# Six transformer layers on one NeuronCore: a loop over layers with two stages becomes one pipeline of 202 steps, and the softmax's maxima and sums are handled in another way

## The reference

```python
def local_attention(q, k, v):          # windows of 32 rows, each sees itself and the one before
    ...
    mask = (it < jb) | (it > jb + w) | (jb == -1)
    sim = jnp.einsum('bhwie,bhwje->bhwij', bq, bk2) * QK_SCALE
    sim = jnp.where(mask, -jnp.finfo(sim.dtype).max, sim)
    attn = jax.nn.softmax(sim, -1)
    out = jnp.einsum('bhwij,bhwje->bhwie', attn, bv2)

def attn_layer(x, Wqkv, qs, ksc, Wo):  # 16 heads of 64
    q, k, v = jnp.split(x @ Wqkv, 3, -1)
    ...
    q = l2norm(q) * qs
    k = l2norm(k) * ksc
    q = q * cos * scale + rotate_half(q) * sin * scale
    k = k * cos * inv + rotate_half(k) * sin * inv
    return local_attention(q, k, v) @ Wo           # (heads put side by side)

def ffn_layer(x, g, bln, W1, b1, W2, b2):          # 341 hidden columns and as many gates
    xn = (x - mu) / jnp.sqrt(var + 1e-05) * g + bln
    a, gate = jnp.split(xn @ W1 + b1, 2, -1)
    return a * jax.nn.gelu(gate, approximate=False) @ W2 + b2

for i in range(6):
    x = attn_layer(shift_tokens(x), ...) + x
    x = ffn_layer(shift_tokens(x), ...) + x
```

## Time and profile before

| | |
|---|---|
| three runs, median (lowest to highest) | 3576.26 us (3575.43 to 3576.86) |
| the profiled execution | 3575.57 us, its span 3573.7 us |
| mean granted TensorE clock | 0.958 of full speed |
| PE busy | 3252.6 us, 91% |
| ACT busy | 2933.6 us, 82% |
| DVE busy | 2791.6 us, 78% |
| POOL busy | 2045.7 us, 57% |
| exponentials (L1321), busy of instruction and accumulator read | 1229.9 and 765.0 us, 3072 each |

### The profile page before, as it was taken

The page is one execution under the profiler, slowest core; times in us unless marked ns, Lnnn a source line. Parts: engine busy times, 40 slices in busy tenths (PEclk is TensorE's granted clock), DMA queues, the critical chain, the costliest instruction groups (busy, mean ns, idle before and its releaser), DMA issues. The chain is left out here.

```text
span 3573.7 us, 118257 instructions
## 1 busy us (share of the span) xinstructions
PE 3252.6 (91%) x42076; PEld 2208.0 (62%) x42076; DVE 2791.6 (78%) x5370; ACT 2933.6 (82%) x9257; POOL 2045.7 (57%) x2150
## 2 busy tenths in 40 slices
PE   5699998889999789999789999978999977999977
PEld 4466665656666556666566666665666655666656
DVE  7788887578888568888658888757888856888865
ACT  3399998479999459999649999937999955999973
POOL 3566665456666356666446666545666634666644
PEclk8799999899999899999899999989999989999999
DMA  2000001100000100000110000010000010000011
GB/s 70 10 7 8 7 7 33 22 13 7 7 7 6 47 15 8 7 7 7 37 24 7 8 7 7 10 44 14 7 8 7 6 43 19 8 7 7 7 34 42
DMA packets 141061, 57.58 MB, mean 16 GB/s; under 512 B 118598, under 2 KB 137668, under 8 KB 139460
## 3 DMA queue, kind: packets, MB, share of 16 engines
q1 hardware_dynamic: 140484, 50.01, 5.9%
HBM read 22.57 MB, written 2.10 MB: 7 GB/s over the span
## 5 line engine op out<-in xcount | busy, mean ns | idle before, releaser
L1321 ACT ACTIVATE probs<-s_ps,nbias,rnorm 128x64 f32<-128x64 f32 x3072 | 1229.9, 447 | 1.6 <-DVE nbias L1039 0.9
L1524 POOL TENSOR_TENSOR qk_rot<-by_cos,by_sin 128x1024 f32<-128x1024 f32 x384 | 914.0, 2380 | 381.9 <-DVE by_sin L989 334.8
L597 PE MATMUL ring<-wvo,xsT 128*32 128x512 f32 x6144 | 794.8, 600 | 10.2 <-ACT vo L1144 10.2
L1321 ACT ACTIVATION_READ_ACCUMULATOR probs<-s_ps,nbias,rnorm 128x1 f32 x3072 | 765.0, 249 | 0.0
L1513 POOL TENSOR_TENSOR probs<-probs,rrow 128x256 f32<-128x256 f32 x768 | 454.6, 613 | 429.1 <-DVE rrow L973 429.1
L986 DVE TENSOR_TENSOR by_cos<-qk_ps,rotary 128x1024 f32<-128x1024 f32 x378 | 463.0, 1225 | 147.1 <-ACT squares L1307 147.1
L1533 POOL TENSOR_TENSOR qk_rot<-qk_rot,rnorm 128x1024 f32<-128x1024 f32 x192 | 365.5, 1904 | 341.4 <-DVE rnorm L733 341.4
L543 PEld LDWEIGHTS ring<-cst,qk_rot 128*128 128x128 f32 x3072 | 341.3, 141 | 243.7 <-ACT vo L1144 155.9
L543 PE MATMUL ring<-cst,qk_rot 128*128 128x128 f32 x3072 | 446.4, 278 | 27.6 <-POOL qk_rot L1524 24.4
L1001 DVE TENSOR_REDUCE sumsq<-squares 128x16 f32<-128x1024 f32 x384 | 462.9, 1206 | 0.0
L989 DVE TENSOR_TENSOR by_sin<-qk_ps,rotary 128x1024 f32<-128x1024 f32 x378 | 459.2, 1215 | 0.0
(11 more groups left out here) (166 smaller groups left out, 5433.4 us busy)
## 6 DMA issues: line engine op xcount, KB each, us to landing
qk_rot<-L_ffn_Wqkv SPq DMA_DIRECT2D x7, 1024.0 KB, 5.1
xs<-x_tok SPq DMA_DIRECT2D x194, 32.0 KB
xs<-x_tok SPq DMA_DIRECT2D x194, 31.8 KB
by_cos<-x_tok SPq DMA_DIRECT2D x48, 128.0 KB
by_cos<-x_tok SPq DMA_DIRECT2D x48, 127.0 KB
wv<-L_ffn_Wqkv SPq DMA_DIRECT2D x7, 512.0 KB, 6.6
wo_pad<-L_ffn_Wo SPq DMA_DIRECT2D x14, 256.0 KB, 7.3
xs<-x_tok SPq DMA_DIRECT2D x194, 0.2 KB
```

What stands on the lines that cost most here:

```text
L597: last = mm(r[WIN * mh:WIN * (mh + 1), :], xsT[:, a, WIN * w:WIN * (w + 1)], wvo[:, mh, :, :], start=True, stop=True)
L1321: last = nc.scalar.activation(probs[:, a, h // 4, :, h % 4, :], s_ps[:, half, c:c + 2 * WIN].rearrange("p (s c) -> p s c", s=2), ACT.Exp, ...
L1524: g.tensor_tensor(qk_rot[:, n, :], by_cos[:, n, :], by_sin[:, n, :], ALU.add).then_inc(added[qk], 1)
```

## The change

The loop over layers goes, and so does the border between the two stages. One list of 202 steps per engine covers 6 x 32 tiles; a tile's attention is spread over steps k to k+3, and the feed-forward work of a group of four tiles is set into the steps that follow its last tile (group(k, f) is the group whose last residual was f steps ago). The next layer's weights are prepared in the steps at the end of the layer before, in buffers of their own (wqk_next, wvo_odd and wvo_even, w1_hi, w1_lo). Layer norm's gain goes into W1 and its offset into the bias b1 (bias_product, biases); group squares are made on POOL (squared4), Gelu writes into hid. All four vo copies and all kT copies are ACT's now. q is scaled by 1/|q| on POOL (normalise_rotated "q"), so that exponentials need no scale; the negated maxima (float32r) are added to the scores by a PE product (shift), and so they need no bias: an instruction takes four heads, 4 a tile. Row sums are reductions on DVE (row_sums). The mask is added in PSUM by DVE (in maxima), except for the first tile of a sequence, which still has a PE product.

The core of the diff; the feed-forward parts keep the operations of before but for what is said above.

```diff
+TILES = DEPTH * NT
+GROUPS = DEPTH * NG
+LAST_RESIDUAL = FT - 1 + 3
+STEPS = LAST_RESIDUAL + FT * (GROUPS - 1) + 8
...
+        def group(k, f):
+
+            u, rest = divmod(k - LAST_RESIDUAL - f, FT)
+            return u if rest == 0 and 0 <= u < GROUPS else None
...
+        NEXT_VALUES = (("wvT0", 14), ("wvT1", 15), ("wvo0", 18), ("wvo1", 19), ("wvo2", 22), ("wvo3", 23))
+
+        def ring_uses(k):
+
+            groups_first = [("b1", layer_at(k, 7)), ("down", group(k, 6)), ("gate2", group(k, 3))]
+            groups_first += [(part, next_layer_at(k, at_step)) for part, at_step in NEXT_VALUES]
+            tiles_first = [("vo2", k - 2), ("qT1", k - 2), ("qT0", k - 2), ("vo1", k - 2), ("kT0", k - 2)]
+            groups_up = [("up0", group(k, 3)), ("up1", group(k, 3))]
+            tiles_next = [("vo0", k - 2), ("kT1", k - 2), ("pT0", k - 3), ("xsT", k)]
+            groups_next = [("xn", group(k, 2)), ("up2", group(k, 4))]
+            tiles_last = [("pT1", k - 3), ("vo3", k - 2), ("o", k - 3)]
+            groups_last = [("gate0", group(k, 2)), ("gate1", group(k, 2))]
+
...
-                every_tile(step, 3)
...
+                    if first:
+                        mm(s_ps[:, half, :], ident_bf[:, :],
+                           mask_bf[:, 0:2 * WIN].unsqueeze(1).broadcast_to([P, 8, 2 * WIN]),
                            start=True, stop=False, skip_group_check=True)
...
+                def shift(half, s):
+
+                    if not there(k, None, s):
+                        return
+                    T = T0 - s
+                    pe.wait_ge(max_done[half], done(T))
+                    mm(s_ps[:, half, :], ident_r[:, :], nmax[:, 8 * half:8 * half + 8].unsqueeze(2)
+                       .broadcast_to([P, 8, 2 * WIN]), start=False, stop=True,
+                       skip_group_check=True).then_inc(shifted[half], 1)
...
+                bias_product(layer_at(k, 7))
+                down(group(k, 6))
+                up("gate", 2, group(k, 3))
+                project("k", 0, 1)
+                project("k", 1, 1)
+                for part, at_step in NEXT_VALUES:
+                    next_values(next_layer_at(k, at_step), part)
+                values(2, 2)
+                transposed("q", 1, 2)
+                transposed("q", 0, 2)
+                values(1, 2)
+                transposed("k", 0, 2)
+                up("up", 0, group(k, 3))
+                up("up", 1, group(k, 3))
+                values(0, 2)
+                transposed("k", 1, 2)
+                probs_transposed(0, 3)
+                xs_transposed(0)
+                scores(0, 2)
+                normalised_transposed(group(k, 2))
+                project("q", 0, 0)
+                project("q", 1, 0)
+                up("up", 2, group(k, 4))
+                probs_transposed(1, 3)
+                values(3, 2)
+                scores(1, 2)
+                shift(0, 2)
+                output(3)
+                up("gate", 0, group(k, 2))
+                up("gate", 1, group(k, 2))
+                shift(1, 2)
+            every_step(step)
...
+                def row_sums(half, s):
+
+                    if not there(k, None, s):
+                        return
+                    T, a, h = T0 - s, (par - s) % 2, slice(8 * half, 8 * half + 8)
+                    dve.wait_ge(exp_done[half], done(T))
+                    p = probs[:, a, 2 * half:2 * half + 2].rearrange("p q s h c -> p q h s c")
+                    v.tensor_reduce(psum_row[:, h].rearrange("p (q h) -> p q h", q=2), p, AXY,
+                                    ALU.add).then_inc(row_summed[half], 1)
+
...
-                        T = T0 - s
-                        dve.wait_ge(s_ready[half], done(T))
-                        v.tensor_reduce(smax[:, 8 * half:8 * half + 8], heads(s_ps[:, half, :], 8), AX,
-                                        ALU.max).then_inc(max_done[half], 1)
...
+                    dve.wait_ge(shifted[half], done(T - 1))
+                    dve.wait_ge(s_ready[half], done(T))
+                    scored = heads(s_ps[:, half, :], 8)
+                    if T % TPB:
+                        v.tensor_tensor(scored, scored, mask_bf[:, 2 * WIN:4 * WIN].unsqueeze(1)
+                                        .broadcast_to([P, 8, 2 * WIN]), ALU.add).then_inc(masked[half], 1)
+                        dve.wait_ge(masked[half], passed(T - T // TPB))
+                    v.tensor_reduce(nmax[:, 8 * half:8 * half + 8], heads(s_ps[:, half, :], 8), AX, ALU.max,
+                                    negate=True).then_inc(max_done[half], 1)
...
+                x_new(group(k, 6))
+                biases(layer_at(k, 7))
+                sum_of_squares("k", 1)
+                row_reciprocals(1, 3)
+                inverse_norms(0, 1, 1)
+                rotate("k", 0, 1)
+                inverse_norms(1, 2, 1)
+                hidden(0, group(k, 3))
+                hidden(1, group(k, 3))
+                rotate("k", 1, 1)
+                xsT_lower(0)
+                normalised(group(k, 2))
+                centre(group(k, 1))
+                inverse_norms(2, 4, 1)
+                maxima(0, 2)
+                inverse_norms(4, 6, 1)
+                hidden(2, group(k, 4))
+                lower(group(k, 2))
+                inverse_norms(6, RSQRT_OPS, 1)
+                rotate("q", 0, 0)
+                maxima(1, 2)
+                rotate("q", 1, 0)
+                row_sums(0, 2)
+                residual(3)
+                group_deviation(group(k, 1))
+                row_reciprocals(0, 2)
+                w1_lower(layer_at(k, 7))
+                sum_of_squares("q", 0)
+                row_sums(1, 2)
+            every_step(step)
...
-                        for h in (h0, h0 + 1):
-                            c = h % 8 * 2 * WIN
-                            last = nc.scalar.activation(
-                                probs[:, a, h // 4, :, h % 4, :],
-                                s_ps[:, half, c:c + 2 * WIN].rearrange("p (s c) -> p s c", s=2), ACT.Exp,
-                                scale=rnorm[:, a, h:h + 1], bias=nbias[:, h:h + 1],
-                                accum_out=psum_row[:, h:h + 1])
...
+                    act.wait_ge(pT_ps[half], done(T - 2))
+                    act.wait_ge(shifted[half], done(T))
+                    for q in range(2):
+                        last = nc.scalar.activation(
+                            probs[:, a, 2 * half + q].rearrange("p s h c -> p h s c"),
+                            s_ps[:, half, 256 * q:256 * q + 256].rearrange("p (h s c) -> p h s c", h=4, s=2), ACT.Exp)
+                    last.then_inc(exp_done[half], 1)
+
...
+                gelu(group(k, 3))
+                square("k", 1)
+                next_wqk_upper(next_layer_at(k, NT), 1)
+                vo_evacuated(2, 2)
+                w1_upper(layer_at(k, 7))
+                for part, at_step in NEXT_VALUES:
+                    next_values(next_layer_at(k, at_step), part)
+                q_evacuated(1, 2)
+                q_evacuated(0, 2)
+                vo_evacuated(1, 2)
+                k_evacuated("low", 0, 2)
+                k_evacuated("high", 0, 2)
+                vo_evacuated(0, 2)
+                xsT_upper(0)
+                k_evacuated("low", 1, 2)
+                p_evacuated(0, 3)
+                k_evacuated("high", 1, 2)
+                normalised_upper(group(k, 2))
+                square("q", 0)
+                next_wqk_upper(next_layer_at(k, NT - 1), 0)
+                p_evacuated(1, 3)
+                xsT_evacuated(0)
+                exponentials(0, 2)
+                vo_evacuated(3, 2)
+                exponentials(1, 2)
+            every_step(step)
...
+
+                normalise(1, 2)
+                add_rotated("q", 0)
+                next_wqk_lower(next_layer_at(k, NT - 1), 0)
+                squared4(group(k, 0))
+                normalise_rotated("q", 0)
+                add_rotated("k", 0)
+                x_and_bias(group(k, 2))
+                normalise_rotated("k", 0)
+                group_rsqrt(group(k, 0))
+                normalise(0, 1)
+                next_wqk_lower(next_layer_at(k, NT - 1), 1)
+                for j in range(TPB):
+                    next_table(next_layer_at(k, NT - TPB + j + 1), j)
+            every_step(step)
```

More of the change, by code:

```diff
@@ L31 @@
 AX = mybir.AxisListType.X
+AXY = mybir.AxisListType.XY
 P = 128
@@ L89, in constants @@
     first[0:WIN, 0:WIN] = NEG
-    parts["mask"] = np.concatenate([first] + [mask] * (TPB // 2 - 1), 1)
-    parts["keep"] = np.tile((np.arange(TPB // 2) > 0).astype(f)[None], (P, 1))
+    parts["mask"] = np.concatenate([first, mask], 1)
     h = np.arange(P) // D0
@@ L316, in schedule, with every_step, there @@
                 step(k, k % 2, None)
-        def every_tile(step, depth, before_last=None):
-            for k in range(NT + depth):
-                if before_last and k == NT + depth - 1:
-                    before_last()
```

(56 more changed lines are left out.)

1350 lines of the change are left out of this document (628 added, 722 removed).

## The result

The changed kernel takes 3738.0 us (median of 4 runs, 3734.9 to 3739.5) where the kernel before takes 3576.5: ratio 1.045, 95% interval 1.043 to 1.047. It is slower by 162 us, and 304 us over the forecast of 3434. The profiled execution has a span of 3735.3 us.

What follows compares the result with a forecast made beforehand. PE was taken as full, with waits on DVE and ACT making 66.5 us per group of four tiles. 48 groups 3192, front 148, borders 60, ends 32 and 1.9 around the span gave 3434 us; range 3240 to 3600.

Steps and rivals of the forecast that it cites:

- plain: Step without feed-forward products on PE: 14.4 us, with PE idle 0.45 while DVE masks, takes maxima and rotates q.
- up 2: Step with feed-forward product up2 (f = 4): like the step without such products plus 0.75 us, 15.1.
- down, xn, gates: Step with down, xn and two gates: 18.5 us on PE plus 0.8 waiting for normalised, 19.3.
- gate 2, up 0, up 1: Step f = 3: 16.2 us on PE plus 1.5 idle behind ACT's Gelu table load and three Gelus, 17.7.
- PE, 13.95 a tile and 63.3 a group: PE's work at old product prices: 13.95 us a tile, plus 7.5 feed-forward per four tiles, 63.3 a group.
- Rival 4: DVE and POOL shut each other out of SBUF, 2.38 us per meeting, one in two tiles: 3660 us; chance 0.12.
- The other waits, 3.2 a group: PE's idle time within a group: 0.45 in steps waiting on DVE, 0.8 for normalised, 1.5 behind ACT's Gelus.
- the forecast's third step: Step f = 3, with gate2, up0 and up1: products wait for ring banks held behind hidden 0 and 1; 1.5 us idle.
- If PE waits longest for ring banks with ACT behind them: Sign that the forecast is wrong: the copies moved to ACT would then be the cost; no size given.
- Rival 3: DVE's mask and row sums at their upper end, 0.6 us more in 7 tiles of 8: 3535 us; chance 0.05.
- Table loads: ACT's two loads a group, 1.28 us each: Gelu's delays the f = 3 step, Exp's fits in ACT's spare time.
- Borders at 12 each: Five layer borders at 12 us, 60 in all, for values, transposes, weight parts and project's waits of about 1 and 4.5.

Runs made afterwards that it cites:

- e4: The changed kernel with POOL's sum of q split into four instructions of 256 columns, DVE's order untouched: 3583.6 us, ratio 1.0025.
- e6: The kernel before with values 0 and the four transposes of k swapped, adding two changes of kind per tile: 3624.5 us, ratio 1.014.
- e12: e7 with k's first half taken first by PE and ACT, and all four POOL passes over q and k in quarters: 3778.3 us, ratio 1.056.
- e11: e4 with half of the output's products left out (output not the reference's): 3510.0 us, 74 less than e4.
- e7: e5's product order, with e4's quartered sum and the norm's blocked int32 step moved ahead of k's first rotation: 3574.0 us, ratio 0.9998.
- e3: The changed kernel with the mask added by PE products in all tiles and none by DVE: 3761.2 us, ratio 1.052.
- e8: e7 with Identity in place of Gelu, so no table loads for it (output not the reference's): 3522.6 us, 51 less than e7.
- e5: The changed kernel with PE's products grouped by kind, 8 changes a tile rather than 12, and a third xsT slot: 3861.9 us, ratio 1.079.

## Why the prediction was wrong

The sign was wrong, and the time lies outside the range (3240 to 3600). By its own steps, with the mean length of each kind of step away from layer borders:

| | plain | up 2 | down, xn, gates | gate 2, up 0, up 1 | group |
|---|---|---|---|---|---|
| forecast | 14.4 | 15.1 | 19.3 | 17.7 | 66.5 |
| changed kernel | 16.9 | 16.6 | 19.5 | 20.7 | 73.8 |
| e4 (fewest edits, L786's long meetings gone) | 16.2 | 16.2 | 19.3 | 18.9 | 70.7 |

The means depend on which steps count as near a border: the group comes to between 72.9 and 74.1 in the changed kernel and 70.0 to 71.1 in e4, so what follows is good to some 40 us. 7.3 us over, times 48, is 350. Front, borders and ends come to 3738 - 48 x 73.8 = 196 us, against 242 (148 + 60 + 32 and 1.9), 46 less. Together 304.

- **PE, 13.95 a tile and 63.3 a group: wrong, too low by 3.4 a group.** The failed step is the assumption that a product costs what it cost in the old order. From medians between starts in e4: 24 transposes 3.07 (forecast 2.61), values 3.88 (3.78), output 1.88 (1.75), the two shifts 0.41 and 0.32 (0.25 each), projections 3.0, scores 2.0, the tokens' 0.2: 14.8 a tile. The feed-forward part is right: 2.60 for down, 0.38 for the transposes, 4.5 for the 18 products, 7.5. So 66.7 a group against 63.3, with no wait in it. e6 shows the cause, the changes of kind, in the kernel before; that the whole 0.85 a tile comes from the six changes more is an estimate (0.14 each).
- **Rival 4, the meetings of DVE and POOL: right in mechanism, wrong in its chance (0.12).** The failed step is "DVE gets there 0.1 to 0.2 us earlier": POOL was 0.02 earlier. A margin of 0.2 us after a whole step laid out from rounded prices is no margin. It meets in 139 tiles, not 96; but e4 takes back 154 us, 1.1 per meeting where I had 2.38, since the steps have some slack. The Trainium skill (SBUF — State Buffer, Who interferes with whom) was the rule that spoke against the change. L786's row agrees with it; e12 goes beyond it, since there a DVE step was shut out for eight POOL instructions, and not for the one that it met.
- **The other waits, 3.2 a group: 4.0 in e4** (70.7 less 66.7). Right in mechanism, in part wrong in place and size. The loop over DVE's mask and maxima is there, at 0.29 us in 69 steps, 21 us in all, for 0.45 in two steps of the four; its own terms (11.7 + 2.62) gave 14.3 and an idle time of 0.37 in place of 0.45. PE's dearer products cover part of it, `down` covers it behind the plain step, and e11 uncovers it. PE's wait for normalised is twice the 0.8 of the forecast, 81.0 / 48 = 1.7 a group, and 1.1 in e4. The banks behind `hid`, in the forecast's third step, were there (59.6 us, a little over 1.2 a group) and are gone from the first rows of e4. "If PE waits longest for ring banks with ACT behind them" was among the signs named. It is near to what e7 shows once PE is quicker: scores wait there for ACT's copies of k, though for the data and not for a bank.
- **Mask and row sums on DVE at 0.6: 0.73 and 0.59** from start to start, as they were priced (0.69 and 0.68 as durations). At the lower end. Rival 3 is out, and by e3 the addition on DVE is 23 us better than the product on PE.
- **Exponentials at 0.3, POOL at 12.4: right.** The row below has the mean; two take 0.66 together, so 0.33 each. POOL is busy for 2430.6 / 192 = 12.7 per tile.

```profile
L1361 ACT ACTIVATE probs<-s_ps 128x256 f32<-128x256 f32 x768 | 252.6, 383 | 219.1 <-PE s_ps L640 218.1
```

- **Table loads: right in size, wrong in the reason.** At most one of the two is on the path (e8, in e7's order), but the second lies behind PE's first shift and not in spare time.
- **Borders at 12 each: too high.** PE waits for the lower parts of wqk for 18.4 us in all, in ten places (last row of PE's waits above), where I had 5.5 for each of five pairs.

How the remaining 200 us of the 350 (those that e4 doesn't take back) divide between PE's dearer work and the waits isn't settled: less PE work alone gives back 44% of itself (e11) or 10 us of 92 (e7 against e4), because the loop over DVE, copies, banks and `xsT_lo` are each a few tenths behind PE. That several chains stand this close is also why no single edit brings the forecast.

The gain expected from one pipeline is real. Before, 3576 - 148 - 192 x 14.03 = 734 us lay outside front and tiles; now it is 48 x 7.5 = 360 of feed-forward work on PE and 48 of borders and ends, 326 less. But the rest of the group is (73.8 - 7.5) / 4 = 16.6 a tile for 14.03, 488 us more in 192 tiles. 488 - 326 = 162, the measured loss.

## What to carry to other kernels

Price a product on PE by its neighbours: where a list mixes stationary widths, count the changes of width and put equal ones together, above all when a schedule is rewritten to interleave more kinds of work. Putting them together pays only as far as the engines behind PE keep up: by itself it lost 124 us here (e5). When a rearrangement lets small DVE instructions run beside long POOL ones, don't settle who comes first by a tenth of a microsecond; either give the small instructions a place where POOL waits for them, or price the meeting as certain. And when one engine is full and the three others are busy for over 60%, work taken off it does not come back whole as time: leave some of it out, as e11 does, before counting on it.

## What the runs showed of the hardware

A change between products with 128 and with 32 stationary columns costs PE time, at a granted clock of 1.00: values take 0.12 us more ahead of transposes, and eight transposes 0.15 more ahead of values; a pair of changes costs 0.257 us a tile in e6. A DVE instruction of 32 columns can be shut out for a run of several POOL instructions, not just for the one that it met: 4.82 us over eight instructions in e12, where another of 32 columns came through between two in e4, e7 and e12. An in-place addition of a bf16 mask to 512 columns of PSUM takes 0.69 us on DVE, and a sum over two axes with a stride 0.68, as long as a plain maximum (0.69).
